# Grouped attention with four filler places in a step, later additions to x, and weight units two earlier

## The reference, cut to what matters

```python
q = (query @ Wq).reshape(b, sq, 32, 32)      # 32 heads of 32 columns
k = (key @ Wk).reshape(b, sk, 8, 32)         # 8 heads, each for 4 heads of q
v = (value @ Wv).reshape(b, sk, 8, 32)
probs = softmax(q @ k.T * 32 ** -0.5)
x = x + tanh(g) * ((probs @ v) @ Wo)
```

## Time and profile before

| | |
|---|---|
| median of 3 runs | 3269.11 us (3264.38 to 3276.44) |
| the profiled execution | 3268.81 us, span 3267.2 us |
| mean granted clock of PE | 0.926 |
| busy: PE, DVE, ACT, POOL | 86%, 62%, 36%, 14% of the span |
| this stage | from 1573 to 2369 us of the span |

### The profile page before, as it was taken

One profiled execution on the slowest core, in us unless ns is written; L12 is line 12 of the kernel. 1 busy time (PEld: TensorE's weight loads), 2 busy tenths in 40 slices (PEclk: granted clock), 3 DMA queues, 4 the chain that ended last, 5 costly groups with the idle time before them and its releaser, 6 DMA issues. The chain is left out here.

```text
span 3267.2 us, 54164 instructions
## 1 busy us (share of the span) xinstructions
PE 2815.7 (86%) x20468; PEld 1974.6 (60%) x20468; DVE 2012.4 (62%) x3515; ACT 1184.0 (36%) x2604; POOL 450.0 (14%) x516
## 2 busy tenths in 40 slices
PE   7999999999994799978689999998668898847988
PEld 4665666566562677845355555555467777736664
DVE  5545544644627666744276677776547788846774
ACT  3333333333332223313154455544345545411222
POOL 0110110111012100000021121112123233200000
PEclk9999999999996899988789999999788899967999
DMA  6100100100106554352333333332250100035441
GB/s 237 44 32 12 44 32 12 44 32 11 38 1 206 166 135 136 111 164 93 124 108 114 127 133 114 121 110 90 49 185 7 36 18 24 18 107 184 163 145 46
DMA packets 103179, 292.18 MB, mean 89 GB/s; under 512 B 33480, under 2 KB 56680, under 8 KB 93456
## 3 DMA queue, kind: packets, MB, share of 16 engines
q1 hardware_dynamic: 75408, 220.09, 20.1%
q0 software_dynamic: 18704, 53.14, 5.4%
q10 hardware_dynamic: 8848, 16.10, 1.9%
HBM read 246.24 MB, written 43.04 MB: 89 GB/s over the span
## 5 line engine op out<-in xcount | busy, mean ns | idle before, releaser
L1828 POOL TENSOR_SCALAR grouped_probs<-grouped_probs,grouped_rsum 112x375 f32<-112x375 f32 x256 | 149.4, 603 | 761.8 <-DVE grouped_rsum L1882 761.8
L1462 DVE TENSOR_REDUCE latent_nmax<-bank 112x1 f32<-112x487 f32 x128 | 85.2, 665 | 269.6 <-PE bank L1327 261.9
L2074 PE MATMUL bank<-ffn_qT,ffn_wgu 128*128 128x112 bf16 x4096 | 218.1, 219 | 22.3 <-ACTq L2145 13.0
L2074 PEld LDWEIGHTS bank<-ffn_qT,ffn_wgu 128*128 128x128 fp8e4 x4096 | 215.3, 101 | 27.1 <-issue 24.6
L1878 DVE TENSOR_REDUCE grouped_nmax<-bank 112x1 f32<-112x375 f32 x256 | 122.4, 541 | 129.0 <-PE bank L1705 127.2
L1288 PEld LDWEIGHTS bank<-latent_hT,latent_wq 128*128 128x128 f32 x1536 | 179.4, 194 | 9.7 <-issue 9.2
L2213 POOL TENSOR_TENSOR ffn_h<-ffn_sl,ffn_us 128x448 f32<-128x448 f32 x64 | 136.1, 2127 | 356.5 <-ACTq L2168 356.5
L1251 POOL TENSOR_SCALAR latent_probs<-latent_probs,latent_rsum 112x487 f32<-112x487 f32 x128 | 88.0, 687 | 659.7 <-DVE latent_rsum L1467 659.7
L1288 PE MATMUL bank<-latent_hT,latent_wq 128*128 128x112 f32 x1536 | 178.5, 277 | 0.0
L1792 ACT ACTIVATE grouped_probs<-bank,grouped_nmax 112x375 f32<-112x375 f32 x256 | 143.3, 572 | 90.4 <-DVE grouped_nmax L1878 90.4
L1266 PE MATMUL bank<-latent_wv,latent_hT 128*125 128x384 f32 (+1 forms) x512 | 168.8, 491 | 0.0
(11 more groups left out here) (398 smaller groups left out, 5767.7 us busy)
## 6 DMA issues: line engine op xcount, KB each, us to landing
grouped_raw<-L_weights SPq DMA_DIRECT2D x24, 2048.0 KB, 8.1
points_spread<-numbers SPq DMA_DIRECT2D x32, 912.0 KB
codes<-grouped_code SPq DMA_DIRECT2D x24, 512.0 KB, 7.4
latent_hT<-ctxT SPq DMA_DIRECT2D x8, 1500.0 KB, 6.9
plain_ctxT<-ctxT POOLq DMA_DIRECT2D x8, 1500.0 KB, 16.2
plain_ctx<-ctx POOLq DMA_DIRECT2D x8, 1500.0 KB, 33.8
grouped_ctxT<-ctxT SPq DMA_DIRECT2D x8, 1500.0 KB, 7.9
latent_xy<-planes SPq DMA_DIRECT2D x8, 1024.0 KB, 8.5
```

What stands on the lines that cost most here:

```text
L1828: pool.tensor_scalar(pr[:, g % 2, j, :], pr[:, g % 2, j, :], rsum[:, g % 2, j:j + 1], 1.0, ALU.mult, ALU.mult)\
L2074: mm = pe.matmul(ahead.tile(t)[:, i * Q:(i + 1) * Q], wgu[:, u0 + f // 4, c:c + P], qT[:, k, :], start=(k == 0), stop=(k == KC - 1))
```

## The change

- The plan has a fourth place, `ahead`, just before part 2 of the transposes. Each k, q and y projection is cut in pieces of 4, 2 and 2 of its 8 matmuls (before: 4 and 4), the middle piece in `ahead`. `output` becomes an item `"o"` of the plan. Step 6 now holds v0 and v1, step 7 v2.
- Steps 2 and 5, in which DVE runs `scaled`, hold no weight tile. `scaled` and `measured` are now the last things that DVE does in their steps (1, 4, 6 and 2, 5, 7), after all rounding.
- The results are added to x in steps 2 and 3, between the rounding of `middle` and the reciprocal. y0 and y1 have a bank each (6 and 7).
- Units run two sooner: units 0 and 1 are done in the negative steps, and the last batch's steps hold 4 tiles in place of 12.
- In the negative steps the projections get banks 0 to 5. `norm.root` for batch 0 stands ahead of everything on ACT. The context of batch 0 is loaded by `memory_ffn` with the early weights, and SP's order follows the new units: weights of unit 0 directly after the load of z.
- `zT` moves from step 2 to the end of step 3, `qT` to `middle` of step 6.

```diff
-    PLAN = [([("k0", 0)], ["w0"], [("k0", 1), "w1"]),
-            ([("y0", 0)], ["w2"], [("y0", 1)]),
-            ([("y1", 0)], ["w3"], [("y1", 1), "zT", "w4"]),
-            ([("k1", 0)], ["w5"], [("k1", 1)]),
-            ([("q0", 0)], ["w6"], [("q0", 1), "w7"]),
-            ([("q1", 0)], [], [("q1", 1), "w8"]),
-            ([("v0", 0), ("v0", 1)], ["w9"], ["qT", "w10"]),
-            ([("v1", 0), ("v1", 1)], ["w11"], [("v2", 0), ("v2", 1)])]
+    N, UNITS = B * QUADS, 3 * B
+    BEGIN, END = -QUADS, N + 4
+    PLAN = [([("k0", 0, 4)], ["w0"], [("k0", 4, 6)], [("k0", 6, 8), "w1", "o"]),
+            ([("y0", 0, 4)], ["w2"], [("y0", 4, 6)], [("y0", 6, 8), "w3", "o"]),
+            ([("y1", 0, 4)], [], [("y1", 4, 6)], [("y1", 6, 8), "o"]),
+            ([("k1", 0, 4)], ["w4"], [("k1", 4, 6)], [("k1", 6, 8), "w5", "o", "zT"]),
+            ([("q0", 0, 4)], ["w6"], [("q0", 4, 6)], [("q0", 6, 8), "w7", "o"]),
+            ([("q1", 0, 4)], [], [("q1", 4, 6)], [("q1", 6, 8), "o"]),
+            ([("v0", 0, 8)], ["qT"], ["w8", ("v1", 0, 4)], [("v1", 4, 8), "o"]),
+            ([("v2", 0, 8)], ["w9"], ["w10"], ["w11", "o"])]
...
+                u = 3 * b + 2 + i // 4
+                return ("w", u, i % 4) if 0 <= u < UNITS else None
...
             for g in range(BEGIN, END):
+                first, middle, ahead, last = PLAN[g % QUADS]
                 if 0 <= g < N:
                     scored(g)
-                do(first, b)
-                if ahead:
+                do(first, g)
+                if 0 <= g - 1 < N:
                     turned(g - 1, 0)
                     turned(g - 1, 1)
-                do(middle, b)
-                if ahead:
+                do(middle, g)
+                do(ahead, g)
+                if 0 <= g - 1 < N:
                     turned(g - 1, 2)
-                do(last, b)
-                if ahead:
-                    output(g - 1)
+                do(last, g)
...
                 if 0 <= g < N:
                     maxima(g)
-                rounded_for(middle, b)
+                rounded_for(middle, g)
+                if r in (2, 3) and 1 <= b <= B:
+                    result(b - 1, r - 2)
                 if 0 <= g < N:
                     sums(g)
...
-                if r in (2, 5) and 0 <= b < B:
-                    scaled(3 * b + (1 if r == 2 else 2))
-                if r in (1, 2) and 1 <= b <= B:
-                    result(b - 1, r - 1)
-                rounded_for(last, b)
-                if r in (1, 4) and 0 <= b < B:
-                    measured(3 * b + (1 if r == 1 else 2))
-                if r == 6 and b + 1 < B:
-                    measured(3 * b + 3)
-                if r == 7 and b + 1 < B:
-                    scaled(3 * b + 3)
+                rounded_for(ahead, g)
+                rounded_for(last, g)
+                if r in (1, 2, 4, 5, 6, 7):
+                    u = 3 * b + {1: 3, 2: 3, 4: 4, 5: 4, 6: 5, 7: 5}[r]
+                    if 0 <= u < UNITS:
+                        if r in (1, 4, 6):
+                            measured(u)
+                        else:
+                            scaled(u)
...
-            grouped = early(two, "grouped", wk="L2_xattn_Wk", wv="L2_xattn_Wv", wq="L2_xattn_Wq", wo="L2_xattn_Wo")
+            grouped = early(two, "grouped", {"ctx0": ([P, KC, CTX], A["ctxT"][0].rearrange("(k p) n -> p k n", p=P))},
+                            wk="L2_xattn_Wk", wv="L2_xattn_Wv", wq="L2_xattn_Wq", wo="L2_xattn_Wo")
```

More of the change, by code:

```diff
@@ L1548, in at, with bank @@
             return (name, n, 0) if name in ("zT", "qT") else (name[0], n, int(name[1]))
-        def step(g):
-            return g // QUADS, PLAN[g % QUADS]
-        BANK = {"k": (6, 6), "y": (6, 6), "q": (6, 6), "v": (6, 6, 6)}
+        def bank(t, g):
+            kind, n, i = t
+            if kind == "w":
+                return 6 if (g % QUADS, i) == (7, 2) else 7
+            if kind == "y":
+                return 6 + i
+            if g < 0:
+                return {"k": (0, 1), "q": (2, 3), "v": (4, 5, 4)}[kind][i]
+            return 6
         order = []
         for g in range(BEGIN, END):
-            b, (first, middle, last) = step(g)
+            first, middle, ahead, last = PLAN[g % QUADS]
             def uses(items):
                 for item in items:
-                    t = at(item, b)
-                    if t is None or (not isinstance(item, str) and item[1] == 1):
+                    t = at(item, g)
+                    if t is None or (not isinstance(item, str) and item[1] > 0):
                         continue
                     if t[0] == "zT":
-                        order.extend([(("zT", t[1], i), 7 - i) for i in range(2)])
+                        order.extend([(("zT", t[1], i), 4 + 2 * i) for i in range(2)])
                     elif t[0] == "qT":
                         order.extend([(("qT", t[1], i), 6 + i) for i in range(2)])
+                    elif t[0] == "o":
+                        order.append((("o", g - 1), 5))
                     else:
-                        order.append((t, 7 if t[0] == "w" else BANK[t[0]][t[2]]))
+                        order.append((t, bank(t, g)))
             if 0 <= g < N:
@@ L1575, in grouped_attention @@
             uses(middle)
+            uses(ahead)
             if 0 <= g - 1 < N:
@@ L1806, in output @@
                 act.drain().then_inc(oT_ready, 1)
+            norm.root(act, 0, 0)
             for g in range(BEGIN, END):
-                b, (first, middle, last) = step(g)
-                ahead = 0 <= g - 1 < N
+                first, middle, ahead, last = PLAN[g % QUADS]
+                b = g // QUADS
                 if 0 <= g < N:
                     exponents(g)
-                if g % QUADS == 1 and b + 1 < B:
+                if g % QUADS == 1 and 0 <= b and b + 1 < B:
                     norm.root(act, 0, b + 1)
-                do(first, b)
-                do(middle, b)
-                if ahead:
+                do(first, g)
+                do(middle, g)
+                do(ahead, g)
+                if 0 <= g - 1 < N:
                     last_tile(g - 1)
-                do(last, b)
-                if ahead:
-                    output(g - 1)
+                do(last, g)
         @block.gpsimd
@@ L1924, in _ @@
             for g in range(BEGIN, END):
-                b, (first, middle, last) = step(g)
-                r = g % QUADS
+                first, middle, ahead, last = PLAN[g % QUADS]
+                b, r = g // QUADS, g % QUADS
                 if 0 <= g < N:
                     maxima(g)
-                rounded_for(middle, b)
+                rounded_for(middle, g)
+                if r in (2, 3) and 1 <= b <= B:
+                    result(b - 1, r - 2)
                 if 0 <= g < N:
@@ L2800, in dram, with early @@
             return nc.dram_tensor(name, shape, dt, kind="Internal").ap()
-        def early(ctx, stage, **weights):
-            return Early(nc, ctx, stage, {n: ([P, A[w].shape[0] // P, A[w].shape[1]], fold(A[w])) for n, w in weights.items()})
+        def early(ctx, stage, more={}, **weights):
+            return Early(nc, ctx, stage, {**more, **{n: ([P, A[w].shape[0] // P, A[w].shape[1]], fold(A[w])) for n, w in weights.items()}})
         idx = dram("nearest", (B, P, KC, 16), U32)
```

98 lines of the change are left out of this document (50 added, 48 removed).

## The result

The changed kernel takes 3233.45 us (median of 4 runs, 3231.93 to 3235.50), the kernel before beside it 3272.78 us (4 runs). The ratio is 0.988 with a 95% interval of 0.9857 to 0.9903: faster by 1.2%, by more than the 0.5% that a measurement of this kernel can tell. The forecast was 3223 us with a range of 3205 to 3246. The profiled execution took 3231.93 us (span 3230.3) against 3268.81 before.

What follows compares the result with a forecast made beforehand. PE was taken to set the pace, waiting 7.75 us a middle batch, mostly for weight tiles rounded behind DVE's long scale work. Terms 2.6 - 32 - 15.5 - 1.4 = -46.3 gave 3223 us, range 3205 to 3246.

Steps and rivals of the forecast that it cites:

- The steady batches: Batches 1 to 6: PE's work unchanged, its waiting less; 84.25 us against 89.6 each, -32 us in six.
- 4.52 and 2.06 us: PE's waits in steps 2 and 5 of a middle batch, forecast to go.
- Step 7: Steady batches: 8.6 us of PE work, `output` waits some 1.0, so 9.6; next maxima about 1.0 late, absorbed by step 0.
- The start: Stage start to first scores: context wait goes, tiles and w4's wait come; first scores at 1634 in place of 1631.8.
- The wait for w4: Start of the stage: PE idle from about 1584 until w4 is rounded at 1594, 10 us.
- The last batch and the end: Last batch -15.5 us with 4 tiles in place of 12; end -1.4, y1 no longer waiting for y0's addition.
- The five bare steps: Last batch, steps 3 to 7 without fillers: 8.4 us each at a low clock, 42 in all, -6.7.
- steps 0 and 1: Last batch, its first two steps: -0.3 us.
- move to the maxima: Rival: DVE late into steps 3, 6 and 0, PE standing before part 2; 88 us a batch, 3245; chance 0.16.
- ten us late: Rival at the stage's start: first weights come late behind x and context in the queue; 3233 us; chance 0.12.
- PE's clock fell in steps 7 and 0: Rival: half rate over 4 to 7 us of work costs 2 to 3.5 a batch; 3235 to 3244; chance 0.06.
- The waits for stores that would have made it slower: Rival: `measured` waits for stored codes, delaying the next maxima; 16 us later gives 3290; chance 0.03. Its DMA wait signals wrong.

Runs made afterwards that it cites:

- C: Changed kernel with w3 and w7 put back into steps 2 and 5, and DVE running `scaled` ahead of their rounding: 3281.54 us, ratio 1.0016.
- B: Changed kernel with w3 and w7 put back at the end of steps 2 and 5, still rounded before `scaled`: 3235.13 us, ratio 0.9879.
- F: Changed kernel with results added to x at the end of steps 1 and 2, ahead of w3's rounding, `measured` and `scaled`: 3258.94 us, ratio 0.996.
- E: Changed kernel without the fourth place; what stood ahead of part 2 of the transposes moves behind it: 3237.18 us, ratio 0.9909.
- G: Changed kernel with step 7 relieved: w8, w9, w10 and pieces of v2 and k0 moved, layer norm statistics behind the rounding: 3202.15 us, ratio 0.9800.
- D: Changed kernel with units not two sooner: none in the negative steps, 12 tiles in the last batch: 3210.67 us, ratio 0.9802.
- H: Changed kernel with three 128x375 matmuls that nobody reads in each of the last five steps: 3214.25 us, ratio 0.9854.
- K: Changed kernel and kernel before, each run again unaltered: stage 751.0 and 795.8 us, outside the stage 2486.3 and 2482.3 us.

## Why the prediction was right, point by point

**The stage.** -46.3 was forecast, -45.5 measured. The median lies 10.5 us over the forecast: 3.7 are the median of before (3272.78, not 3269.11), and the rest is about what lies outside the stage, where I had counted nothing: +8.6 in the two profiled runs, against a spread of 31 us. That the sum came so near is partly luck: terms below were off by up to 4.3 us, in both directions.

**The steady batches,** -29.8 for -32. The mechanism held for the waits: steps 2 and 5 lost their 4.52 and 2.06 us. But it is only half of the gain. The sum took PE's work as the same and only its waiting as changed; over the six batches, before and changed (windows), PE's idle time falls by 15.6 us (40.0 to 24.4) and its busy time by 14.2, the mean clock going from 0.98 to 1.00:

```profile
1716.10:2254.50 538.40, 498.37 (x3652) 308.00 (x3648) 381.27 (x715) 266.52 (x636) 110.15 (x192) 0.98 0.34 117
1719.90:2228.50 508.60, 484.18 (x3656) 303.26 (x3651) 378.12 (x715) 269.43 (x637) 113.35 (x192) 1.00 0.35 124
```

That -29.8 stands so near to -32 is therefore luck in part. Of the plan, C shows what matters (rounding ahead of `scaled`), B that the place alone is worth 0.5 us, F that the results must be out of DVE's way. The reading of the 4.52 us was too simple, though: in batch 4 only 2.23 of them are waits for a rounded tile. Another 0.55 stand before part 2, and 1.75 before the second half of zT, which waited for DVE to add y to x (timeline of the kernel before):

```profile
2019.98 0.60 PE L516 MATMUL bank<-const_ident,grouped_z 112*128 112x112 f32 x4 [1.75 <-DVE grouped_x L1899]
```

The change moves zT too, and no run moves it back alone. Two terms of the sum were off and cancelled in part. PE's waits are 4.4 us a batch, not 2.0; and in batch 4, at full clock, the busy time is 80.5 us, not 81.75 plus the 0.5 that I had added for changes of work. By E the fourth place has most of that difference; the rest of the 14.2 goes with the clock, which I had not counted. Step 7 was the worst: I had DVE 1.0 late into step 0 and `output` waiting 1.0; PE waits 1.26 for w10's rounding and 0.70 for `output`, and 0.86 in step 0 (w0 and w1). In step 6 it waits 0.95 us as forecast, but for w8's rounding and not for ACT's copy of q turned. G took 2.9 of these 4.4 back.

**The start,** -2.1 for +2.2. The first scores stand at 1634.0, to the tenth where I had put them, by luck: the stage itself began 4.3 us later. Counted from its load of x the start took 56.3 us and not 60.5. The wait for w4 was 8.5 for 10, since unit 0 was there 1 us sooner than forecast by that count; the other waits 3.3 for 3; the work 44.4 for 47.5, at a clock of 0.89 where the old 42.5 had been read at 0.84. The first step lost 2.8 to `scaled` of unit 2 (2.5 forecast), and batch 0 took 1.5 more for 0.4. What I did not ask is what the start would cost without the units, and D gives it: 40.4 us. I had summed the gain of the context and the cost of the units to nearly nothing, and never put the part against its own gain.

**The last batch and the end,** -15.2 for -16.9. The eight steps took 73.4 us for 86.7, -13.3 for -15.5, and the end 1.9 less for 1.4. The five bare steps were near: 7.4, 8.5, 8.1, 8.5 and 8.9 against 8.4 each, at a clock of 0.50 to 0.85 as in the earlier trace rows. H shows that the clock is the reason. The term that failed is steps 0 and 1: forecast 0.3 shorter, they took 22.2 us for 19.3, at clocks of 0.84 and 0.85. And the gain is only in part that of the units: D, with 12 tiles in the last batch, already has 7.7 of the 15.2, since its step 2 takes 9.9 us as well, not 18.6.

**The rivals.** The wait didn't move to the maxima: from 1720 to 2228 us, in all six middle batches, no wait of PE before part 2 is listed. Unit 0 was not ten us late. PE's clock fell in steps 7 and 0 only once: from 1668.4 to 2142.8 us it is 1.00 throughout, with three tiles and 2.0 us of waiting in every step 7, and then, where step 7 of batch 5 ends and batch 6 begins, it is 0.50 for some 3 us; in the second profile of the same kernel (K) not even there. So the rival cost under 2 us, but C, with a lower clock in many places, shows how near it was. By the rule of the Trainium skill on transposes (TensorE: Matmul & The Clock Gate, Part 4: PE-mode transpose) it would have come; the trace, with one fall in six batches, doesn't bear that out here. It tests the rule weakly, since of PE's 8.1 busy us in step 7 only 3.5 are transposes. The waits for stores that would have made it slower came once, 3.73 us of DVE before `measured` at 1616, ahead of the first scores. By the prediction's own words that was a sign of being wrong, but PE didn't wait for it.

## What to carry to other kernels

Where one engine feeds filler work to the bound engine, the order inside the feeder counts most (C, 7.4 us a batch), and then the slot (B 0.5, G 2.9 with an order of its own): short results that somebody waits for go ahead of long work that nobody waits for, and an addition whose input comes late goes a step later. Price every part of a change against its own gain; one that loses can hide behind ones that win. Compare the stage that was edited as well as the whole, and run the same kernel twice, before a few us of the whole are put down to an edit. A time in the span can agree with a forecast by luck; count it from the start of its stage.
